# Scatters and gathers of the first expert layers: paced by their own landings, in place of by events of TensorE

## The reference

```python
capacity = int(T / E * CAP_FACTOR)                 # 160 slots for each of 8 experts
probs = softmax(x @ Wr)
topk_probs, topk_experts = top_k(probs, 2)         # two experts for each token
pos_all = cumsum(onehot, axis=1) - onehot          # place of a token in its expert's queue
keep = pos < capacity
buf = buf.at[e_flat, b_idx, pos_c].add(x_rep * keep)
h = relu(einsum('ebnc,ech->ebnh', buf, W1) + b1)   # 128 -> 512
y = einsum('ebnh,ehc->ebnc', h, W2) + b2           # 512 -> 128
y_tok = y[e_flat, b_idx, pos_c] * keep * p_flat
out = y_tok.reshape(B, T, K, C).sum(axis=2)
```

## Time and profile before

| | |
|---|---|
| time, median of 3 runs | 1464.06 us (1462.74 to 1464.46) |
| span of the profiled execution | 1486.9 us |
| TensorE busy | 1437.6 us (97%) |
| VectorE busy | 1065.3 us (72%) |
| ScalarE busy | 917.8 us (62%) |
| GpSimd busy | 280.4 us (19%) |
| chain that ended last: TensorE | 87% |
| chain: issue, and another core or an unknown queue | 2% and 2% |

### The profile page before, as it was taken

The page is one execution under the profiler, slowest core; times in us unless marked ns, Lnnn a source line. Parts: engine busy times, 40 slices in busy tenths (PEclk is TensorE's granted clock), DMA queues, the critical chain, the costliest instruction groups (busy, mean ns, idle before and its releaser), DMA issues.

```text
span 1486.9 us, 43341 instructions
## 1 busy us (share of the span) xinstructions
PE 1437.6 (97%) x18426; PEld 1023.7 (69%) x18426; DVE 1065.3 (72%) x2172; ACT 917.8 (62%) x1727; POOL 280.4 (19%) x325
## 2 busy tenths in 40 slices
PE   7999789999999999999999999999999999999996
PEld 6988774566677675667777756577777565677486
DVE  6884037888666678886766788876666887787754
ACT  5774466666666666566666666666666666666542
POOL 4164613013210012130000120400001214000055
PEclk9999999999999999999999999999999999999999
DMA  8501221001110011010000110110101101101002
GB/s 223 196 20 53 68 65 39 22 23 46 30 29 16 16 42 32 23 48 16 17 16 16 41 32 22 35 33 17 30 16 39 32 23 34 34 16 30 1 19 58
DMA packets 44464, 58.30 MB, mean 39 GB/s; under 512 B 8231, under 2 KB 32656, under 8 KB 44144
## 3 DMA queue, kind: packets, MB, share of 16 engines
q1 hardware_dynamic: 35120, 38.27, 9.4%
q0 software_dynamic: 9152, 17.26, 4.4%
HBM read 22.14 MB, written 19.32 MB: 28 GB/s over the span
## 4 chain that ended last, share of the span: by engine, by line
PE 87%; DVE 5%; ACT 3%; issue 2%; another core or an unknown queue 2%; DMA 0%; DVEq 0%; ACTq 0%
PE bank L1153 29%; PE bank L1166 28%; PE bank L1076 6%; PE bank L1081 4%; PE bank L1090 4%; PE bank L412 2%; PE bank L446 2%; PE bank L1308 2%; PE bank L1304 2%; DVE nmx L1188 1%; PE bank L1265 1%; ACT hT L542 1%; PE bank L830 1%; DVE stats L1349 1%
## 5 line engine op out<-in xcount | busy, mean ns | idle before, releaser
L1197 ACT ACTIVATE prob<-bank,nmx 128x1024 f32<-128x1024 f32 x512 | 570.2, 1114 | 420.3 <-DVE nmx L1188 408.5
L1188 DVE TENSOR_REDUCE nmx<-bank 128x1 f32<-128x1024 f32 x512 | 626.2, 1223 | 200.2 <-PE bank L1153 182.3
L1166 PE MATMUL bank<-prob,vsc 64*64 64x512 f32 x4096 | 644.9, 590 | 1.9 <-DVE ctxT L1215 1.4
L1153 PE MATMUL bank<-q,k 64*64 64x512 f32 x2048 | 527.6, 591 | 3.1 <-ACT prob L1197 1.9
L1153 PE MATMUL bank<-q,ks 64*64 64x512 f32 x2048 | 526.3, 590 | 0.0
L1166 PEld LDWEIGHTS bank<-prob,vsc 64*64 64x64 f32 x4096 | 237.3, 133 | 119.4 <-issue 47.1
L1076 PE MATMUL bank<-xT,wqkv_sb 64*64 64x256 f32 (+1 forms) x1560 | 211.7, 434 | 0.0
L1153 PEld LDWEIGHTS bank<-q,ks 64*64 64x64 f32 x2048 | 139.1, 133 | 75.9 <-issue 21.0
L1760 POOL DMA_INDIRECT yg<-yslots,row_ring x64 | 64.9, 1014 | 609.2 <-PE bank L1153 579.8
L1153 PEld LDWEIGHTS bank<-q,k 64*64 64x64 f32 x2048 | 135.3, 133 | 37.6 <-issue 8.6
L1076 PEld LDWEIGHTS bank<-xT,wqkv_sb 64*64 64x64 f32 x1560 | 92.2, 133 | 86.6 <-issue 36.5
(11 more groups left out here) (270 smaller groups left out, 1628.6 us busy)
## 6 DMA issues: line engine op xcount, KB each, us to landing
ks<-k SPq DMA_DIRECT2D x62, 256.0 KB
yslots<-slots_sb SPq DMA_DIRECT2D x7, 640.0 KB, 3.6
slots_sb<-xslots SPq DMA_DIRECT2D x5, 640.0 KB, 4.5
xslots<-xhat_r POOLq DMA_DIRECT2D x5, 512.0 KB, 7.0
yslots<-xhat_r POOLq DMA_DIRECT2D x5, 512.0 KB, 12.3
w_sb<-in_w SPq DMA_DIRECT2D x1, 2048.0 KB, 9.2
wqkv_sb<-in_wqkv SPq DMA_DIRECT2D x1, 2048.0 KB, 19.0
xslots<-xhat_r,row_s POOLq DMA_INDIRECT x112
```

Source lines behind the costliest of these rows:

```text
L1153: ins = nc.tensor.matmul(bank[rows(c), SC[h][n], :], kk[r, cols(2 * j + c, HD)], qst[pi % 2][r, cols(n, HALF)], start=True, stop=True)
L1166: ins = nc.tensor.matmul(bank[rows(h), CX[n], :], vsc[s][rows(r), rows(h)], prob[g % 3][h][rows(r), cols(n, HALF)], start=(j == 0 and firs ...
L1188: nc.vector.tensor_reduce(nmx[:, 2 * s + h:2 * s + h + 1], bank[:, SC[h][0]:SC[h][0] + 2, :], mybir.AxisListType.XY, ALU.max, negate=True) ...
L1197: nc.scalar.activation(prob[g % 3][h][:].rearrange("p (n c) -> p n c", c=HALF), bank[:, SC[h][0]:SC[h][0] + 2, :], ACT.Exp, bias=nmx[:, 2 ...
```

## The change

- Scatters and gathers no longer wait for events of TensorE. Each waits for the landing of the transfer two in front of it in the same batch; for that the semaphores `f_sc` and `f_gq` are split, by batch and quarter, and into even and odd transfers. The 16 scatters of batch 2 (beside the fourth gated attention) go in threes instead: before each third one GpSimd waits until all those before have landed.
- All 16 scatters of batch 1 are issued before the places of batch 2; GpSimd's bias addition for row 3 stands between the eighth and the ninth. The slots of batch 2 go into a buffer of their own, `row_s2`, without a wait.
- The positions of batch 3 move on TensorE from the third expert of batch 1 to before its first; TensorE waits for `f_kept` at the third expert's products (e == 2) in place of the sixth's. VectorE writes batch 3's slots directly into `row_s`, which replaces the copy on GpSimd.
- Whoever waited for all of a batch's scatters waits for its two semaphores.

```diff
-        f_gq = [sem(f"f_gq{q}") for q in range(4)]
+        f_gq = [[sem(f"f_gq{q}{i}") for i in range(2)] for q in range(4)]
...
+        f_sc = {m: [sem(f"f_sc{m}{i}") for i in range(2)] for m in (1, 2, 3)}
...
-                if e == 5 and m == 1:
+                if e == 2 and m == 1:
                     pe.wait_ge(f_kept, 3)
...
-                if e == 3:
-                    positions(pe, 3, POS_F)
                 if e == E - 1:
-                    pe.wait_ge(f_kept, 3)
                     slots_ahead_tensor(pe, 2, slots2, AHEAD[:2])
...
+        def rows_to(m):
+            return row_s2 if m == 2 else row_s
...
-            if m > 1:
-                p.wait_ge(f_sc, 256 * (m - 1))
-            nc.gpsimd.tensor_copy(row_s[:], skip[:]).then_inc(f_idx, 1)
+            nc.gpsimd.tensor_copy(rows_to(m)[:], skip[:]).then_inc(f_idx, 1)
...
-            nc.vector.tensor_tensor(skip[:], rowf[:], skip[:], ALU.add).then_inc(f_plc, 1)
+            for done in f_sc[1]:
+                v.wait_ge(done, 128)
+            nc.vector.tensor_tensor(rows_to(m)[:], rowf[:], skip[:], ALU.add).then_inc(f_idx, 1)
...
+                if m == 2 and c > 0 and c % 3 == 0:
+                    hold(p, f_sc[m][0], 16 * ((c + 1) // 2))
+                    hold(p, f_sc[m][1], 16 * (c // 2))
+                elif m != 2 and c > 1:
+                    hold(p, f_sc[m][c % 2], 16 * (c // 2))
...
-                    beside_expert(p, 11 + 2 * q + k)
                     for t in (2 * q, 2 * q + 1):
+                        n = 4 * q + 2 * k + t % 2
+                        if n > 1:
+                            hold(p, f_gq[(n - 2) // 4][n % 2], 16 * ((n - 2) % 4 // 2 + 1))
...
-            scatter_in_attention(p, 1, 3)
-            scatter_in_next(p, 1)
+            hold(p, f_idx, 2)
+            scatter(p, 1, range(FIRST))
+            bias_gpsimd(p, 3)
+            scatter(p, 1, range(FIRST, 2 * T))
             place_gpsimd(p, step, 2)
-            scatter_in_attention(p, 2)
-            scatter(p, 2, [13, 14, 15])
-            p.wait_ge(f_plc, 1)
-            p.wait_ge(f_sc, 256 * 2)
-            nc.gpsimd.tensor_copy(row_s[:], skip[:]).then_inc(f_idx, 1)
+            hold(p, f_idx, 3)
+            scatter(p, 2, range(2 * T))
             hold(p, f_idx, 4)
-            for i in range(8):
-                beside_expert(p, 3 + i)
-                scatter(p, 3, [2 * i, 2 * i + 1])
+            scatter(p, 3, range(2 * T))
...
+            positions(pe, 3, POS_F)
             experts_tensor(pe, 1, first_batch_tensor(pe), (a_res, 10), following=slots2)
```

More of the change, by code:

```diff
@@ L132, in bass_hybrid @@
         f_kept = sem("f_kept")
-        f_plc = sem("f_plc")
         f_xs, f_ha, f_ya, f_ys = (sem(n) for n in ("f_xs", "f_ha", "f_ya", "f_ys"))
-        f_sc, f_ld, f_st, f_comb = (sem(n) for n in ("f_sc", "f_ld", "f_st", "f_comb"))
+        f_sc = {m: [sem(f"f_sc{m}{i}") for i in range(2)] for m in (1, 2, 3)}
+        f_ld, f_st, f_comb = (sem(n) for n in ("f_ld", "f_st", "f_comb"))
         f_ga = [sem("f_ga0"), sem("f_ga1")]
-        f_gq = [sem(f"f_gq{q}") for q in range(4)]
+        f_gq = [[sem(f"f_gq{q}{i}") for i in range(2)] for q in range(4)]
         f_gb = [sem("f_gb0"), sem("f_gb1")]
@@ L271, in route_norm_scalar @@
             elif k == 2:
-                a.wait_ge(f_sc, 256)
+                for done in f_sc[1]:
+                    a.wait_ge(done, 128)
             for half in range(2):
@@ L354, in bass_hybrid @@
         row_s = sb("row_s", [P, 2, T], U32, stack=stage_f)
+        row_s2 = sb("row_s2", [P, 2, T], U32, stack=stage_f)
         slots_sb = sb("slots_sb", [P, ST, P], stack=stage_f)
@@ L656, in first_answers_vector @@
             for q in range(4):
-                v.wait_ge(f_gq[q], 64)
+                for done in f_gq[q]:
+                    v.wait_ge(done, 32)
                 for k in range(2):
@@ L669, in scatter @@
                 k, t = c // T, c % T
-                nc.gpsimd.indirect_dma_start(out=xslots[:, :], out_offset=bass.IndirectOffsetOnAxis(ap=row_s[:, k, t:t + 1], axis=0),
-                                             in_=route_rows(m - 1)[:, t, :], in_offset=None,
[L672 to L710, removed]
+                if m == 2 and c > 0 and c % 3 == 0:
[3 more added lines that the diff above has]
+                    hold(p, f_sc[m][c % 2], 16 * (c // 2))
+                nc.gpsimd.indirect_dma_start(out=xslots[:, :], out_offset=bass.IndirectOffsetOnAxis(ap=rows_to(m)[:, k, t:t + 1], axis=0),
+                                             in_=route_rows(m - 1)[:, t, :], in_offset=None,
+                                             bounds_check=B * SLOTS - 1, oob_is_err=False).then_inc(f_sc[m][c % 2], 16)
+        FIRST = 8
         def gather(p, step, m, b):
@@ L1415, in f_norm_vector @@
                 else:
-                    v.wait_ge(f_sc, 256 * (B - 1))
+                    for done in f_sc[B - 1]:
+                        v.wait_ge(done, 128)
                 xhat_vector(v, c0, fb, xhat_r, piece - 5, g_xhat)
@@ L1992, in _ @@
                     store_slots(sp, 1, 0)
-                hold(sp, f_sc, 256 * m)
+                for done in f_sc[m]:
+                    hold(sp, done, 128)
                 hold(sp, f_ld, 16 * m)
```

5 lines of the change are left out of this document (3 added, 2 removed).

## The result

The changed kernel takes 1480.61 us (median of four runs, 1478.71 to 1482.08), the kernel before beside it 1463.40 us (four runs, 1461.79 to 1464.46). The ratio is 1.0117, with a 95% interval of 1.0102 to 1.0131: slower by some 17 us. The forecast was 1468.5 with a range up to 1474. The direction was right, the size four times too small (4.4 us).

A forecast was written before the change was run, and what follows sets the result against it. GpSimd's chain of batch 3's places, scatters and gathers, then VectorE's normalisation, was taken to bound a stall-free kernel of 1464 us. Gate waits +2.3 and late landings +2.1 gave +4.4, so 1468.5 us, range 1455 to 1474.

The forecast's parts named there:

- late landings: Gated transfers beside four 640 KB loads or stores land later and push those behind: 0.5 us each, +2.1, bounds 0 to +6.
- The gate's arithmetic: GpSimd's scatters and gathers wait for landings of 2.0 and 2.45 us plus 0.82 release; last gather 186.4, not 184.1: +2.3 us.
- Late signals only in one profiled execution: TensorE's signals, some 5 us late between 114 and 218 us, belong nearly wholly to the profile, not the timed runs: 22.8 us.
- 7 us around it: Time of a timed run outside its span, added to a stall-free span of 1457 us to give 1464.
- stall-free line: Kernel before laid out without late signals, pair attention's input turned at 191.5 us, not 211.95; the change was compared with it.
- Batch 2's slots "covered": Batch 2's last scatter starts at 137.8, its slots are loaded by 145, TensorE wants them at 148: no cost.
- Idle time at L497: TensorE waits 6 us at the turn for the pair attention (L498 before the change).
- Rival 3: Low clock after TensorE's 6 us idle at L498 adds 3 us; with more late landings 1473 to 1478 us; chance 0.07.
- Rival 1: Late signals of TensorE are real and the gate ends them: -13.5, 1450.5 us, half of the stalls about 1459; chance 0.25.

The follow-up runs named there:

- group A: Sessions in which the kernel before the change takes 1463 us; what sets them apart is not known.
- almost unpaced forms: Four kernels issuing transfers almost without a pause: before without GpSimd's waits for TensorE, changed without gates, that with late positions, three in front; 1511 to 1521 us in group B.
- group B: Sessions in which the kernel before the change takes 1485 to 1490 us; what sets them apart is not known.
- the earlier trace: First profile of the unchanged kernel before, made ahead of the prediction; span 1486.9 us, like group B.
- the scatters' gate alone: Changed kernel with the gathers' waits for earlier landings taken out and the scatters' kept: 1468.75 us, group A.
- three in front: Changed kernel, every scatter and gather waiting for the landing three back instead of two (batch 2: instead of threes): 1459.93 us in group A, 1515.5 to 1521.2 in group B.
- ungated form: Changed kernel with the waits for earlier landings taken out of both scatters and gathers: 1458.44 us in group A, 1516.64 in group B.

## Why the prediction came out as it did

**What bounds the kernel: right.** The chain on GpSimd is the last thing to be ready; TensorE waits for `xhat` at L497, and nothing after it moves.

**In short.** The time left its range by two terms that were too small, both in GpSimd's chain: the late landings (+2.1 forecast, 7.6 measured) and the gate's arithmetic (+2.3). Against the chain of before in group A, the last gather starts 201.10 - 186.07 = 15.0 us later, where the two terms have 4.4. In the order of the chain: batch 3 starts 2.7 us earlier (forecast 4.2), its scatters take 6.5 us more (forecast 1.8), and the gathers 11.3 more (forecast 4.7).

**Late signals only in one profiled execution: wrong, though it did no harm to the sum.** The profiles of the almost unpaced forms in group B show them again, and the kernel before is 22 to 27 us slower in that group's timed runs. Its two profiles differ by 16.5 us up to L498 (211.95 and 195.44) and by 8.9 us after it. That all of this is the late signals is likely, not shown. The 22.8 us between the profiled span and the median were the distance between two groups. The step of this part that failed is "7 us around it": the time of a run is its span and 1.7 to 2.4 us in every run (1478.71 and 1477.0), and the stall-free span was 1461.5, not 1457, so 1457 plus 7 agreed with 1464 by chance. Since the times to be forecast were of group A, the stall-free line was still the one to work on.

The Trainium skill (NOTIFIC — the notification-queue block, 7.1) has the block's internal path hold its producer back rather than lose a record; when the ring behind it is full, a mode decides between that and dropping records. Nothing here decides whether that is what holds TensorE: every timed run also has a span and a granted clock on record, so there is no run without records to compare with.

**The gate's arithmetic (+2.3): right in kind, too small.** From the forecast's last gather at 186.4, which has the late landings not yet in it, to the measured 201.10 it is 14.7 us:

| part of the chain | forecast | measured | missing |
|---|---|---|---|
| batch 2, first scatter | 110.9 | 112.76 | 1.9 |
| batch 2, first to last | 26.9 | 28.35 | 1.4 |
| batch 3, first to last | 21.0 | 25.7 | 4.7 |
| last scatter to first gather | 2.1 | 2.1 | 0 |
| gathers, first to last | 24.2 | 30.9 | 6.7 |

The landings behind it were 2.0 and 2.45 in the forecast, and 2.10 to 2.26 and 2.55 to 2.95 in the chain of waits. The 2.0 was SyncE's issue at +2.24 less a guessed 0.24 for its own issue; the guess was worth 0.1 to 0.25 us a step. The Trainium skill (DMA: Bandwidth & Descriptors, Anatomy of one DMA) has a fixed 2.0 us, and its formula gives an estimate of 0.15 more for 64 KB; the scatters agree (2.10 to 2.26), the gathers do not (2.55 to 2.95). With landings 0.15 and 0.25 longer, the threes give 0.8 us, batch 3 gives 1.1 and the gathers 1.8, so about 3.7 of the 14.7. Of the rest, the next term has 7.6 and the later start of batch 2 has 1.9: batch 1's last scatter starts at 105.02 in place of 104.2, and from the first operation of the places to the first transfer it is 112.76 - 106.01 = 6.75 us in place of 5.7. Of the 1.5 that are left 0.3 is the release, which took 0.84 to 0.95 us in the waits of batch 2 in place of 0.82; the others are not assigned.

```profile
105.02 0.97 POOL L678 DMA_INDIRECT xslots<-xhat_r,row_s  x1 [0.30 <-issue]
106.01 0.34 POOL L622 TENSOR_TENSOR rowmat<-tmp,rowbase 128x64 f32<-128x64 f32 x1
...
112.76 1.04 POOL L678 DMA_INDIRECT xslots<-xhat_r,row_s  x1 [0.86 <-POOL row_s L635]
```

**Late landings (+2.1, bounds 0 to +6): the term that was mis-sized most.** The four steps beside a 640 KB transfer cost, over a plain landing (2.2 and 2.6), 3.97 - 2.2 = 1.8, 3.15 - 2.2 = 0.95, 4.84 - 2.6 = 2.2 and 5.20 - 2.6 = 2.6: 7.6 us in all, against 2.1. I took 0.4 to 0.5 each from the one row in which a gather's landing beside a store was seen from outside; that was the quarter's last transfer, issued well after the store began. The four that start from 0.2 us ahead of a large one to 0.84 us behind it all land after it (the earlier trace rows has 4.5 us for a 640 KB load). The upper bound of 1.5 each was below the measured value for three of the four.

**Batch 2's slots "covered": wrong, and batch 3's were not asked about.** With batch 2's last scatter at 141.11 in place of 137.8, the load into `vact` is issued at 144.66 and TensorE waits 1.56 us. Of that issue 1.3 us is one thing more: it comes 3.55 us after the last scatter's start, not 2.24, and what delayed it is open. For `state` TensorE waits 4.79 us and runs at 1.2 GHz after it. This moved TensorE's own arrival at L497 to 210.67 - 11.40 = 199.3, in place of 191.5 (before in group A: 193.1). It cost nothing, because the chain was later still; with the scatters' gate alone the two came level (idle of only 0.24 at L497).

**Idle time at L497.** Forecast 6 us, measured 11.4, with a turn of 2.05 us. But before waits there too (2.35 us) and turns as slowly, at the same granted clock of 0.50, so the low clock there is no loss of the change. Rival 3, at 1473 to 1478 us, came nearer to the time than the forecast: the later landings in it are what the rows show, the low clock is not. The idle time of that length near was VectorE's; TensorE's own gaps between 122 and 127 us, ahead of the low clock in the earlier trace rows, were of 0.44 to 0.72 us.

**Rival 1, the gate ends the late signals: half true.** It does end them between 60 and 260 us, in the group where they occur, and a gate of three in front does not (ScalarE waits up to 13.75 us "remote" there). The price of 1450.5 us was wrong, since the gate's own waits fill the same time: 1492 us where before has 1486.

**Left open.** What makes the two groups: the sessions name their chips by number, and one number occurs in both groups, so I can't say whether it is the chip, its machine or the hour. Whether the ungated form's 5 us in group A come from the early positions or from the free pace. And how three in front, where almost no wait is ever felt in group A, differs for TensorE from two in front in group B: only that the steady 1.28 us a transfer is broken was seen, not why it matters. No form tried is the best in both groups: ungated 0.9965 and 1.018, three in front 0.9985 and 1.018 to 1.021, before 1 and 1.

## What to carry to other kernels

A wait for the landing n transfers back costs, at every step, what landing and release outlast n steps; so take the landing from transfers that start beside the largest neighbours in the chain (here 5.2 us, not 2.6), and go one further back where it is close (against the ungated form, two in front, with batch 2 in threes, cost 22 us in group A and three in front about 2). Before a profile is set against a set of times, compare its span with the times of runs whose spans are known: the gap of 23 us here was that between two groups of sessions; in one TensorE does not wait for `xhat` before the pair attention, in the other it does. And a pace that looks like idle time in one place may be what keeps TensorE running in another, so it is timed in both before it is removed.

## What the runs showed of the hardware

- Indirect transfers of 64 KB from GpSimd: 1.28 us a scatter and 1.30 a gather if nothing waits; two in front, about 3.1 and 3.4 to 3.7 us a pair. After the landing the waiting transfer starts 0.83 to 0.95 us later (in the chain 145.49 + 3.97 = 149.46, and the next scatter at 150.31).
- One beside a 640 KB transfer of SyncE's landed 1 to 2.6 us later in the changed kernel, and with the gate the transfers behind it wait with it.
- In group B a run of 16 such transfers without waits breaks up TensorE's issue (gaps of 0.3 to 1.1 us between products, up to 14.18 us of waiting for others), and its granted clock has a mean of 0.68 over 25 us; in the changed kernel it is 1.00 there. In group A neither happens, with the same instructions.
